# The first pair's queries and keys placed on chip by the projection stage, and mixing's first rows fetched in the experts' stage

## The reference

```python
x = layernorm(x + block_sparse_attention(x, Wq, bq, Wk, bk, Wv, bv))   # 16 heads of 16, blocks of 64
x = layernorm(x + shared_gelu_mlp(x) + top2_of_8_gelu_experts(x))
x = layernorm(x + time_mix_then_channel_mix(x))                        # a scan over all tokens inside
x = layernorm(x + top2_of_8_gated_experts(x))                          # capacity 640 tokens per expert
```

## Time and profile before

| what | value |
|---|---|
| median of 3 runs | 1872.55 us (1872.14 to 1872.62) |
| the profiled execution, its own time | 1870.89 us |
| its span, first to last instruction | 1869.1 us |
| PE busy | 1634.1 us, 87% of the span |
| mean granted TensorE clock | 0.938 of 2.4 GHz |
| DVE, ACT, POOL busy | 1173.2, 919.1, 607.0 us |

### The profile page before, as it was taken

The page is one execution under the profiler, slowest core; times in us unless marked ns, Lnnn a source line. Parts: engine busy times, 40 slices in busy tenths (PEclk is TensorE's granted clock), DMA queues, the critical chain, the costliest instruction groups (busy, mean ns, idle before and its releaser), DMA issues. The chain is left out here.

```text
span 1869.1 us, 35581 instructions
## 1 busy us (share of the span) xinstructions
PE 1634.1 (87%) x12958; PEld 1368.3 (73%) x12958; DVE 1173.2 (63%) x2482; ACT 919.1 (49%) x2016; POOL 607.0 (32%) x561
## 2 busy tenths in 40 slices
PE   8879999999994688899999498899983699999991
PEld 6777777777773478588888254589982699999991
DVE  7767667777666676555555488666657455555543
ACT  4217787777784443533333365544430344444434
POOL 3420000000042554677775154233320322222121
PEclk9989999999996899999999699999995699999996
DMA  8891434432315601244443621001114223333315
GB/s 287 289 144 46 64 71 82 82 62 63 55 47 192 237 34 46 53 72 74 72 71 48 155 57 42 1 24 46 46 53 151 43 80 95 88 96 83 83 16 180
DMA packets 143784, 164.90 MB, mean 88 GB/s; under 512 B 70794, under 2 KB 115968, under 8 KB 143616
## 3 DMA queue, kind: packets, MB, share of 16 engines
q1 hardware_dynamic: 107248, 111.47, 22.5%
q0 software_dynamic: 28544, 47.35, 12.0%
q10 hardware_dynamic: 7824, 3.81, 1.4%
HBM read 104.75 MB, written 61.08 MB: 89 GB/s over the span
## 5 line engine op out<-in xcount | busy, mean ns | idle before, releaser
L830 DVE TENSOR_REDUCE att_neg_max<-att_m_ps 128x1 f32<-128x320 f32 x496 | 216.9, 488 | 106.3 <-PE att_m_ps L550 103.9
L1929 PE MATMUL silu_h_ps<-silu_xT,silu_w_part 128*128 128x320 f32 x1536 | 236.4, 312 | 1.2 <-DVE silu_xT L2025 0.9
L1929 PEld LDWEIGHTS silu_h_ps<-silu_xT,silu_w_part 128*128 128x128 f32 x1536 | 227.0, 189 | 2.6 <-DVE silu_xT L2025 1.3
L550 PE MATMUL att_m_ps<-att_k,att_q 96*128 96x384 f32 x496 | 183.5, 384 | 8.1 <-DMA att_q<-qk 6.1
L1894 POOL DMA_INDIRECT summed<-silu_y,all_table x40 | 63.6, 1590 | 256.1 <-DVE silu_y L2065 149.6
L948 POOL DMA_DIRECT2D att_q<-att_max_row x40 | 20.2, 506 | 380.9 <-DVE att_max_row L838 379.0
L1655 POOL DMA_INDIRECT part<-layer_xT,all_table x72 | 118.7, 1648 | 59.9 <-DVE layer_xT L1776 50.2
L550 PEld LDWEIGHTS att_m_ps<-att_k,att_q 96*128 96x128 f32 x496 | 95.0, 191 | 38.7 <-issue 18.1
L1941 PE MATMUL silu_y_ps<-silu_w_part,silu_h_part 128*128 128x256 f32 x960 | 116.5, 283 | 2.2 <-DVE silu_w_part L2041 2.2
L1941 PEld LDWEIGHTS silu_y_ps<-silu_w_part,silu_h_part 128*128 128x128 f32 x960 | 115.9, 192 | 2.5 <-DVE silu_w_part L2041 2.5
L1684 PE MATMUL gelu_h_ps<-gelu_wu_part,gelu_xT 128*128 x402 | 110.1, 409 | 2.7 <-DVE gelu_wu_part L1783 2.5
(11 more groups left out here) (315 smaller groups left out, 4002.3 us busy)
## 6 DMA issues: line engine op xcount, KB each, us to landing
experts_w<-in_dram SPq DMA_DIRECT2D x24, 1024.0 KB
qk<-qkv_part POOLq DMA_DIRECT2D x32, 512.0 KB, 4.8
att_k<-qk SPq DMA_DIRECT2D x192, 64.0 KB, 2.4
att_q<-qk SPq DMA_DIRECT2D x168, 64.0 KB, 4.0
v<-qkv_v POOLq DMA_DIRECT2D x8, 544.0 KB, 6.2
att_v<-v SPq DMA_DIRECT2D x8, 544.0 KB, 5.4
qkv_x<-in_dram SPq DMA_DIRECT2D x8, 512.0 KB, 4.9
rows<-att_context SPq DMA_DIRECT2D x8, 512.0 KB, 5.4
```

What stands on the lines that cost most here:

```text
L550: nc.tensor.matmul(bank[:, 0:2 * LOCAL].rearrange("p (a n) -> p a n", a=2), q[b][0:MROW, x, :], local_and_global(b, x), start=True, stop=T ...
L830: ins = nc.vector.tensor_reduce(neg_max[b][:, x - 1:x], bank[:, 0:LOCAL + 2 * BLK], AX.X, ALU.max, negate=True)
L1929: mm = nc.tensor.matmul(h_ps[u % 2][a][:, :], w12_part[f % RING][wp][:, a, k, :], xT[s][xp][:, k, rows], start=(i == 0), stop=(i == 3 * KD ...
```

## The change

It has two parts.

1. The buffers `q0` and `k0` of pair 0 are allocated before the projection. During the projection SP copies each slice of pair 0 from `part[j]` into them, chip to chip, 3 transfers of 32 KB for each `part[j]` (6 for `j` 2 and 3 in the first and the last group, for the end blocks), so 96 + 12 of them. Before that POOL writes the zeros and ones of `q0` and `k0`. `part[j]` now also waits for these copies (`placed[j]`). POOL no longer writes the 16 rows of pair 0 to DRAM: its transfers cover 112 partitions and not 128. `load_x(g + 2)` stands in SP's list between the copies of group `g - 1` and of group `g`. Attention begins without any load of pair 0; SP loads the values and then pair 1. DVE no longer clears `q[0]`, ACT no longer issues queries. POOL does the global keys, the first row of maxima and only then the clearing for pair 1. PE has `idle_products(8)` at the start and `idle_products(2)` after each product of the lead.
2. The expert stage's end is extended: SP loads the four decay columns and ACT computes `ew` and `eu` there. When all additions to `part` have landed, SP and ACT issue 6 transfers each that fetch groups 0 and 1 of mixing into the upper half of `x`, a buffer that is now allocated ahead and also holds the raw `wd` of the experts. POOL no longer waits for the additions. In mixing SP begins with the five weights; ACT takes one root of a constant first.

```diff
+            sp.wait_ge(place_cleared, 4)
+            for g in range(NGRP):
+                if g + 2 < NGRP:
+                    load_x(g + 2)
+                for j in range(4):
+                    t, a = j // 2, j % 2
+                    sp.wait_ge(low_done, 4 * g + j + 1)
+                    for i, h in enumerate((0, 0, 1) if t == 0 else (0, 1, 0)):
+                        r = 48 * a + HD * i
+                        of = part[j][0:HD, h, :].bitcast(F32)
+                        if t == 0:
+                            sp.dma_start(q0[r:r + HD, GB * g:GB * (g + 1), a * BLK:(a + 1) * BLK].bitcast(F32),
+                                         of.rearrange("f (l t) -> f l t", t=BLK)).then_inc(placed[j], 16)
+                            continue
+                        sp.dma_start(k0[r:r + HD, g * GRP:(g + 1) * GRP].bitcast(F32), of).then_inc(placed[j], 16)
+                        if g in ENDS_OF:
+                            to = T if g == 0 else T + BLK
+                            sp.dma_start(k0[r:r + HD, to:to + BLK].bitcast(F32), of[:, ENDS_OF[g]:ENDS_OF[g] + BLK]
+                                         ).then_inc(placed[j], 16)
             finish_prefetch(sp)
+            for j in range(4):
+                sp.wait_ge(placed[j], 16 * places(NGRP - 1, j))
...
                     if i > 0:
                         dve.wait_ge(part_out[j], 16 * i)
+                        dve.wait_ge(placed[j], 16 * places(i - 1, j))
...
-            dst = qk_d.rearrange("t h (g p) n -> p t h g n", p=P)
+            own = slice(HD, P)
+            dst = qk_d.rearrange("t h (g p) n -> p t h g n", p=P)[own]
+            nc.gpsimd.memset(q0[0:3 * 2 * HD, 0:NBLK // 2, :].bitcast(U32), 0).then_inc(place_cleared, 1)
+            nc.gpsimd.memset(q0[0:3 * 2 * HD, NBLK // 2:NBLK, :].bitcast(U32), 0).then_inc(place_cleared, 1)
+            nc.gpsimd.memset(k0[0:3 * 2 * HD, T + 2 * BLK:T + 3 * BLK].bitcast(F32), 0.0).then_inc(place_cleared, 1)
+            nc.gpsimd.memset(k0[3 * 2 * HD:3 * 2 * HD + 1, :].bitcast(F32), 1.0).then_inc(place_cleared, 1)
...
-            load_globals(0)
-            for c in range(CHUNKS):
-                load_keys(0, c)
             load_values(0)
-            sp.wait_ge(kg_in, 96)
             load_globals(1)
             for c in range(CHUNKS):
-                sp.wait_ge(qk_in[c], 192)
                 load_keys(1, c)
-                sp.wait_ge(cleared[1], c + 1)
+                sp.wait_ge(cleared, c + 1)
                 load_queries(sp, 1, c)
...
-            idle_products(36)
-            pe.wait_ge(padded, 2)
-            pe.wait_ge(o_cleared, 1)
+            idle_products(8)
             for n in range(LEAD):
                 for at in range(len(M[n])):
                     maxima(0, n, at)
-                    idle_products(1)
+                    idle_products(2)
+            pe.wait_ge(padded, 1)
+            pe.wait_ge(o_cleared, 1)
...
-            for c in range(CHUNKS):
-                act.wait_ge(cleared[0], c + 1)
-                load_queries(act, 0, c)
...
-            for c in range(CHUNKS):
-                nc.vector.memset(q[0][:, c * CB:(c + 1) * CB, :].bitcast(U32), 0).then_inc(cleared[0], 1)
...
+            copy_globals(0)
+            lay_row(0, 0)
+            pool.wait_ge(globals_copied, COPIES)
+            nc.gpsimd.memset(k[1][0:MROW, T + 2 * BLK:T + LOCAL].bitcast(F32), 0.0).then_inc(padded, 1)
+            for c in range(CHUNKS):
+                nc.gpsimd.memset(q[1][0:MROW, c * CB:(c + 1) * CB, :].bitcast(U32), 0).then_inc(cleared, 1)
+            nc.gpsimd.memset(k[1][MROW:ROWS, :].bitcast(F32), 1.0).then_inc(ones_set, 1)
...
+        def all_added(eng):
             for i in range(YS):
-                pool.wait_ge(y_out[i], 16 * (NT // YS))
+                eng.wait_ge(y_out[i], 16 * (NT // YS))
+
+        @block.sync
+        def _(sp):
+            next_decays(sp)
+            all_added(sp)
+            next_tokens(sp, 0)
...
+            next_decays(act)
+            all_added(act)
+            next_tokens(act, 1)
...
-            load(0)
             for i, a in enumerate((WkT, WvT, WrT)):
                 sp.dma_start(w[:, i], a.rearrange("(k p) n -> p k n", p=P)).then_inc(w_in, 16)
-            load(1)
             sp.dma_start(wo[:, :, :], WoT.rearrange("(k p) n -> p k n", p=P)).then_inc(w_in, 16)
             sp.dma_start(scale_row[:, :], row(scale).broadcast_to([P, D])).then_inc(w_in, 16)
-            for k in range(KD):
-                for a, b in ((td, decay), (tf, first_share)):
-                    sp.dma_start(a[:, k:k + 1], b[k * P:(k + 1) * P].rearrange("(p a) -> p a", a=1)).then_inc(w_in, 16)
...
             act.wait_ge(eps_set, 1)
+            nc.scalar.activation(first[:, :], eps[:, 0:1], ACT.Sqrt)
             step(-2)
-            act.wait_ge(w_in, NW)
-            nc.scalar.activation(e1[:, :], td[:, :], ACT.Exp).then_inc(e1_done, 1)
-            nc.scalar.activation(eu[:, :], tf[:, :], ACT.Exp)
-            act.wait_ge(e1_done, 1)
-            nc.scalar.activation(ew[:, :], e1[:, :], ACT.Exp, scale=-1.0).then_inc(shares_done, 1)
...
+            def next_tokens(eng, a):
+                for g in range(2):
+                    first = TT // 2 + GT * (2 * g + a)
+                    for at, js, piece in token_pieces(part, a, g):
+                        eng.dma_start(x[at, first + js.start:first + js.stop, :], piece).then_inc(first_in[g], 16)
```

More of the change, by code:

```diff
@@ L70, in scratch_rows, with token_pieces, project_qkv @@
     return a[bass.ds(g * GRP, GRP), :].rearrange("(p j) d -> p j d", j=GT)
-def project_qkv(nc, hsT, WqT, bq, WkT, bk, WvT, bv, qk_d, v_d, prefetch, finish_prefetch):
+def token_pieces(part_d, a, g):
+    low, high = slice(0, BLK), slice(BLK, P)
+    of = [scratch_rows(part_d[a * T:(a + 1) * T, :], i) for i in range(NGRP)]
+    own = GT if g < NGRP - 1 else GT - 1
+    pieces = [(high, slice(0, own), of[g][low, 0:own, :]), (low, slice(1, GT), of[g][high, 0:GT - 1, :])]
+    if g > 0:
+        pieces.append((low, slice(0, 1), of[g - 1][high, GT - 1:GT, :]))
+    else:
+        pieces.append((low, slice(0, 1), of[NGRP - 1][low, GT - 1:GT, :]))
+    if g == NGRP - 1:
+        pieces.append((high, slice(GT - 1, GT), of[g][high, GT - 1:GT, :]))
+    return pieces
+def project_qkv(nc, hsT, WqT, bq, WkT, bk, WvT, bv, qk_d, v_d, prefetch, finish_prefetch, q0, k0):
     with ExitStack() as ctx:
@@ L102, in project_qkv, with places @@
         v_out = m.sem("v_out")
+        placed, place_cleared = [m.sem(f"placed{j}") for j in range(4)], m.sem("place_cleared")
         w_high, w_low, x_high, x_low = (m.sem(a) for a in ("w_high", "w_low", "x_high", "x_low"))
         NB = 5 * 16
+        GB = GRP // BLK
+        ENDS_OF = {0: 0, NGRP - 1: GRP - BLK}
+        def places(i, j):
+            return 3 * (i + 1) if j < 2 else 3 * (i + 1 + sum(g <= i for g in ENDS_OF))
         block = ctx.enter_context(nc.Block())
@@ L316, in attend @@
         kg_in, v_in, ones_set = m.sem("kg_in"), m.sem("v_in"), m.sem("ones_set")
-        cleared = [m.sem(f"cleared{i}") for i in range(2)]
+        cleared = m.sem("cleared")
         vg_cleared, globals_copied = m.sem("vg_cleared"), m.sem("globals_copied")
@@ L977, in _ @@
             pool.wait_ge(vg_cleared, 1)
+            copy_globals(0)
[5 more added lines that the diff above has]
+            nc.gpsimd.memset(k[1][MROW:ROWS, :].bitcast(F32), 1.0).then_inc(ones_set, 1)
+            pool.wait_ge(ones_set, 1)
             for p in range(PAIRS):
-                copy_globals(p)
-                for h in range(PARTS):
+                if p > 0:
+                    copy_globals(p)
+                for h in range(1 if p == 0 else 0, PARTS):
                     lay_row(p, h)
@@ L2072, in _, with mix_tokens @@
             experts(dve, work)
-def mix_tokens(nc, part_d, ident, WkT, WvT, WrT, WoT, decay, first_share, scale, x, share, xT2,
+def mix_tokens(nc, part_d, ident, WkT, WvT, WrT, WoT, ew, eu, shares_done, scale, x, first_in, share, xT2,
                WfcT, WmlpT, mlp_scale, wf_part, wm_part):
@@ L2675, in network @@
         tile_expert = m.sb("tile_expert", [P, TILES0], I32)
+        xT = m.sb("xT", [P, KD, T])
+        pair = ExitStack()
+        first_pair = Mem(nc, pair, "first_pair")
+        q0, k0 = first_pair.sb("q0", [P, NBLK, 2 * BLK], F32R), first_pair.sb("k0", [P, T + 3 * BLK], F32R)
+        qk = scratch("qk", 2, 2, D, T)
+        v = scratch("v", PAIRS, P, TT, 2 * VW)
+        project_qkv(nc, hidden_T, Wq, bq, Wk, bk, Wv, bv, qk, v, tables, lambda sp: sp.wait_ge(loaded, 32),
+                    q0, k0)
+        attend(nc, qk, v, hidden, ident, rows[0], part[T:2 * T, :], xT, q0, k0)
+        pair.close()
+        tokens = ExitStack()
+        x = Mem(nc, tokens, "layer").sb("x", [P, TT, D])
         with ExitStack() as layer:
             m0 = Mem(nc, layer, "layer0")
-            xT = m0.sb("xT", [P, KD, T])
-            attend(nc, qk, v, hidden, ident, rows[0], part[T:2 * T, :], xT)
```

(17 more changed lines are left out.)

89 lines of the change are left out of this document (39 added, 50 removed).

## The result

The median is 1893.21 us (1891.79 to 1897.46, 4 runs) against 1872.35 us of the kernel before on the same chip: a ratio of 1.0116 (95% interval 1.0098 to 1.0133). I had forecast 1859.5 us in a range of 1851 to 1868. The time lies 33.7 us above the forecast and 25 us above the range.

The account below looks back on a forecast made before the run. PE, busy 87% of the span, bounds most stages; waits before attention's first score and at mixing's start can go. Terms -9.6 + 1.5 + 4 - 8.9 = -13.0 us gave 1857.9, plus 1.7 for the median: 1859.5 us, range 1851 to 1868.

Parts of the forecast that it names:

- Part 3: The projection itself, with SP's added copies in each group: +4 us, between 0 and +12.
- part 2: The projection's tail, SP's last copies after the last half is ready: +1.5 us, bounds 0 and +2.5.
- the first of part 3: SP's list in the projection: twelve copies and one input take 6.5 us of a group's 8.81, so it keeps up.
- One more term of part 3: Projection's input load_x(3), issued at about 23.4 us behind group 0's copies, takes 5.2 us: 1 us late at most, once.
- A term that I put at nothing: POOL's clearings at the projection's start, about 11 us, end before its first write beside the first loads: no cost.
- The upper bound: Projection: slices at 114 GB/s hold the DMA engines 3.4 us a group, 10.8 us a group with inputs: +12 us together.
- the lower bound: Projection: POOL's packets pass while slices wait, as a share of 1.05 suggests packets of several queues open: 0 us.
- The port rule: Projection's copies: 16 partitions reach 4 of 16 ports, so an estimated 109 GB/s, a quarter of 436.
- The copies land too late: Rival, projection: landing above about 9 us in every group makes the kernel slower; at 13 us, 1904 us. Chance 0.08.
- Part 1: Attention's lead, start to first score: 41.3 us falls to 31.7, -9.6 us, bounds 8 to 11 us gained.
- the second product: Second idle product per unit of attention's lead: pace 0.60 us; without it the lead would gain 8 us more.
- Part 4: Mixing's start: data and weights ready earlier, PE starts at about 1046.3 in place of 1055.20, -8.9 us, bounds -5 and -10.

Follow-up runs that it names:

- Experiment 6: Changed kernel with POOL's writes of the parts carrying 32 of 512 columns in the loop, the rest written once behind the last group: 1920.28 us.
- experiment 1: Only the change at the experts' end and mixing's start, with projection and attention of the kernel before: 1867.83 us, ratio 0.9966 of before.
- 11: Mixing's change alone on the projection and attention of before, without the idle product between two units of attention's lead: 1872.34 us.
- 12: Mixing's change alone on the kernel before, with mixing's five weight transfers issued by ACT and not SP: 1874.64 us, ratio 1.0015 of before.
- 3: Changed kernel without the 60 on-chip copies of pair 0's keys: 1884.27 us.
- Experiment 5: Changed kernel with all 96 copies of slices kept, each moving 32 columns in place of 512: 1895.18 us.
- experiment 10: Changed kernel with one idle product between two units of attention's lead in place of two: 1883.01 us.

## Why the prediction was wrong

**Part 3 failed, and part 2 with it.** The projection's last half came 32.0 us later, where I had +4, and its tail grew from 6.5 to 11.7 us, where I had +1.5. The step that failed is the first of part 3: "six slices of queries at 3.30 / 6 = 0.55 us and six of keys at 0.45 us with one input are 6.5 us of 8.81: it keeps up." A copy costs about 0.95 us of SP's list in the mean, so 12 of them and an input are about 12 us, and 13 in the middle of the stage. Experiment 6 splits this: with POOL's writes of the parts small, an entry of the list costs 0.75 us in place of 0.96, the least is 0.60, and 25.4 of the 32.0 us are gone. One more term of part 3 fails by the same price: the input that I had issued at about 23.4 us and "1 us late at most, once" was issued at 34.32, and ACT waited 12.6 us for it.

I took both prices from stretches in which no large write was under way. They differ in everything else: the DMA share was 0.06 in the first stretch and 1.36 in the second, with 12 and 143 GB/s, so a high share alone doesn't make an issue dear. The trace of before also had dear issues of such slices, ACT issuing ten of queries in 97.75 to 114.29 us while SP issued keys:

```profile
97.75 16.54 ACTq L437 DMA_DIRECT2D att_q<-qk  x10
```

That is 1.65 us each, behind 14 others that had taken about 0.5 us each, and no large write was under way. The first four of the ten took 1.06 to 1.17 us each before the load of the values (544 KB) was issued at 101.96, the dearest of all 3.85 us after it. So a backlog of slices alone already doubled the price. I used the landing time of those transfers for a rival and never their issue.

**A term that I put at nothing cost 1.5 us.** "POOL's clearings (about 11 us) end before its first write, and lie beside the first loads: nothing." The first tile's halves are ready at 14.96 us and not 13.42; in the other profiles without these clearings (experiments 1, 11 and 12) it is 13.2 to 13.3, and with a further clearing (3 and 5) 16.2. A copy of 128x2 numbers on DVE, for which ACT's next rounding waits, took 0.16 us before; now it ends with POOL's last clearing, both at about 11.5 us:

```profile
7.85 3.67 POOL L299 MEMSET first_pair_k<- 1x4288 f32 x1
9.63 1.92 DVE L263 COPY qkv_b_colq<-qkv_b_col 128x2 f32<-128x2 f32 x1
```

**The upper bound was no bound.** My +12 came from bytes over a rate, as if engines served copies and writes in a fixed total. Experiment 5 refutes that: a sixteenth of the bytes costs nearly the same. The delay is one for each copy. For the lower bound I had read the share of 1.05 as packets of two queues at once; in 28 to 32 us every packet is of POOL's own queue (104.6%), so that row says nothing of two queues. The Trainium skill (DMA: Bandwidth & Descriptors, "Queues, rings and completion order") says that an engine goes round its queues packet by packet and drains one before it turns to the next. By that rule a slice of any size waits behind a packet of POOL's write, and the direction fits experiments 5 and 6. The size doesn't follow: in 12 to 115 us of the changed kernel POOL's queue has 4941 packets that take 55.2% of 16 engines' time, an estimate of 0.18 us for one, and the dearest issue takes 1.9 us more than the cheapest. No run here looks into an engine, so this mechanism is argued and not shown. Shown is what makes the copies dear, and not how. The port rule that I weighed is about the rate of bytes, and decided nothing here.

**The rival that came near was right in direction only.** "The copies land too late" needed landings above 9 us. They landed in 5.0 (queries) and 3.3 us (keys) in the median, 6.7 at most, about what I allowed. It was the issue that was late, which I had in no rival. I had given "slower" 0.10 in all, too little for a stage whose DMA engines stood at 1.01.

**Part 1 was right.** 32.6 us against 31.7; spacing 0.625 against 0.60; and the remark that the second product gives back 8 us was right too (8.8 in experiment 10). The gain of 8.7 us is measured from one profile of before, and the lead of before takes up to 44.2 us in others.

**Part 4 had the right mechanism and two terms too small.** As I had assumed, there is no shift of mixing: 8.93 us from the last addition's issue to mixing's first instruction, 9.01 before. But the weights needed 9.3 us from their last issue (1070.69 to 1079.95) where I took 5.3. My 5.3 was the landing of a small column of decays and not of weights, and the third group's loads follow at once; which of the two makes the difference is not shown. DVE got its data 1.7 us after the start and not 0.3. The gain is 5.8 us in the changed kernel, 7.1 in experiment 1 and 7.9 in experiment 10, against 8.9.

**The sum** of what was measured is +37.1 - 8.7 - 5.8 = +22.6 us, the difference of the spans. Smaller shifts between the stages cancel. From the router's start to the experts' first output product are 143.8 us before, 145.7 in the changed kernel and 147.4 in experiment 1, but 144.0 in experiments 10 and 12 with the same code there, so this comes from one execution to another and not from the change.

## What to carry to other kernels

Price an issue where it will stand, beside the large writes of that stage, and not by a stretch without them: the same copy took 0.59 and 2.50 us within ten us. Count the added transfers and not their bytes, and look for the slowest issue of such a transfer in the trace. When a queue's list is full, ask also what stands behind it: here the next input. An order on one queue protects what stands first on it; before moving transfers to a second queue, ask what used to be behind them.

## What the runs showed of the hardware that I had not expected

- Issuing a copy of 16 rows from chip to chip took 0.59 us when little else moved and up to 2.50 us beside POOL's writes, and its price hardly changed when it carried 2 KB in place of 32.
- With half of these copies moved to ACT's queue, or left out, the median issue of the queries that SP kept rose from 0.72 us to 1.10 and 1.00.
- More buffers made it slower: attention starts at 133.4 us with eight, at 125.3 with four.
- Five weights that landed 8.0 us after their last issue, with the next loads behind them on the same queue, took 15.9 us with those loads beside them on another.
- A DVE copy of 128x2 numbers took 1.92 us and ended with POOL's clearing, where it took 0.16 us alone.

The version that beats both kernels is experiment 1: 0.9966 of before.
